# Dealing PSUM's eight banks anew: two for scores and four for the ring, in place of three and three

## The reference, cut to what matters

```python
mod = (silu(c) @ wmod).reshape(4, 6, 1, -1)
sa, ca, ga, sb, cb, gb = (mod[:, i] for i in range(6))      # ga, gb kept at least 0.25 from zero
h = layernorm(x) * (1 + ca) + sa
qkv = (h @ W_qkv + b_qkv), split by head into q, k, v
q, k = rope(q), rope(k)
att = softmax(causal(q @ k.T / sqrt(32)))
x = x + ga * ((att @ v) @ W_proj + b_proj)
h = layernorm(x) * (1 + cb) + sb
x = x + gb * ffn(h)
```

## Time and profile before

| what | value |
|---|---|
| runs: median (lowest to highest of 3) | 3261.88 us (3260.14 to 3275.57) |
| profiled execution: its own time, its span | 3263.36 us, 3261.6 us |
| mean granted TensorE clock | 0.969 |
| TensorE busy | 3008.8 us, 92% |
| VectorE busy | 2491.3 us, 76% |
| ScalarE busy | 1842.8 us, 57% |
| GpSimd busy | 1586.5 us, 49% |

### The profile page before, as it was taken

How to read it: one execution, slowest core, us unless ns; L and a number is a source line. 1 busy time by engine, 2 the same in 40 slices (tenths; PEclk the granted TensorE clock), 3 DMA queues, 4 the chain that set the end, 5 groups by cost and what they waited for, 6 DMA issues and landing times.

```text
span 3261.6 us, 59116 instructions
## 1 busy us (share of the span) xinstructions
PE 3008.8 (92%) x21664; PEld 1157.1 (35%) x21664; DVE 2491.3 (76%) x4214; ACT 1842.8 (57%) x3651; POOL 1586.5 (49%) x1586
## 2 busy tenths in 40 slices
PE   3699999999999999999999999999999999999896
PEld 1324343434343332434333243433424333342222
DVE  4597777777768788777877878777887878878477
ACT  2406565786655555786555555587555555455541
POOL 2303435382516556272654726366472645627355
PEclk8759999999999999999999999999999999999997
DMA  5403030413031120413114031321314122031121
GB/s 209 110 1 73 14 77 14 99 43 73 17 99 38 47 78 27 103 45 84 44 43 104 30 96 34 68 65 32 97 33 118 40 49 67 28 78 46 56 79 61
DMA packets 180875, 205.27 MB, mean 63 GB/s; under 512 B 21460, under 2 KB 137428, under 8 KB 179428
## 3 DMA queue, kind: packets, MB, share of 16 engines
q1 hardware_dynamic: 180584, 201.50, 23.1%
HBM read 114.09 MB, written 36.50 MB: 46 GB/s over the span
## 4 chain that ended last, share of the span: by engine, by line
PE 41%; issue 20%; DVE 13%; POOL 11%; POOLq 7%; ACT 3%; DVEq 2%; DMA 2%; SPq 1%; ACTq 1%
PE ring L1171 8%; PE ps_out L1221 8%; DVE mpart L911 8%; PE ps_scores L1207 7%; POOL psum L538 5%; PE ps_scores L1145 5%; PE ps_den L1238 4%; PE ps_den L1244 3%; POOL psum L537 3%; PE ring L1193 2%; PE ps_scores L1157 2%; POOLq L573 2%; POOLq L511 2%; POOLq L565 1%; ACT prob L739 1%
## 5 line engine op out<-in xcount | busy, mean ns | idle before, releaser
L739 ACT ACTIVATE prob<-ps_scores 128x512 f32<-128x512 f32 (+3 forms) x2560 | 1251.8, 537 | 950.1 <-PE ps_scores L1210 457.6
L911 DVE TENSOR_REDUCE mpart<-ring 128x1 f32<-128x512 f32 (+3 forms) x2560 | 1406.3, 599 | 356.6 <-PE ring L1171 191.0
L1171 PE MATMUL ring<-qk 96*128 96x512 f16 (+3 forms) x2560 | 875.0, 364 | 64.6 <-DVE mpart L911 46.7
L1207 PE MATMUL ps_scores<-qk 98*128 98x512 f16 (+3 forms) x2560 | 861.9, 350 | 44.4 <-ACT prob L739 36.2
L537 POOL TENSOR_TENSOR psum<-prob 128x512 f32<-128x512 f32 x360 | 480.6, 1335 | 387.2 <-ACT prob L739 305.7
L1221 PE MATMUL ps_out<-prob,v 128*32 128x512 f32 (+3 forms) x5120 | 602.0, 542 | 0.0
L1171 PEld LDWEIGHTS ring<-qk 96*128 96x128 f16 x2560 | 235.5, 98 | 857.6 <-DVE mpart L911 590.2
L538 POOL TENSOR_TENSOR psum<-prob 128x512 f32<-128x512 f32 x360 | 480.4, 1334 | 0.0
L1207 PEld LDWEIGHTS ps_scores<-qk 98*128 98x128 f16 x2560 | 245.8, 98 | 362.7 <-ACT prob L739 227.1
L1145 PE MATMUL ps_scores<-hT,wg 128*128 128x512 f16 x1536 | 346.1, 382 | 4.6 <-POOL hT L528 3.5
L556 POOL TENSOR_TENSOR xs<-xs,bc 128x512 f32<-128x512 f32 x60 | 81.0, 1350 | 432.0 <-DMA xs<-in_L_attn_x_dram 430.7
(11 more groups left out here) (128 smaller groups left out, 2581.9 us busy)
## 6 DMA issues: line engine op xcount, KB each, us to landing
qk<-half SPq DMA_DIRECT2D x384, 128.0 KB, 3.5
turn<-in_rope_dram SPq DMA_DIRECT2D x64, 512.0 KB, 4.6
xs<-in_L_attn_x_dram SPq DMA_DIRECT2D x124, 256.0 KB, 2.8
attn_out_T<-ot SPq DMA_DIRECT2D x63, 256.0 KB, 2.2
otin<-attn_out_T SPq DMA_DIRECT2D x30, 512.0 KB, 4.5
out_dram<-x SPq DMA_DIRECT2D x60, 256.0 KB, 2.1
wg<-w_qkv_halves SPq DMA_DIRECT2D x16, 768.0 KB, 5.1
qk<-in_L_wmod_dram SPq DMA_DIRECT2D x1, 6144.0 KB, 26.8
```

The source lines that it names most:

```text
L739: act.activation(prob[:, s % 3, p, h % 2, 0:w], ps_scores[(HG * s + h) % NBK][:, 0:w], ACT.Exp, scale=SCALE).then_inc(exp_done, 1)
L911: dve.tensor_reduce(mpart[:, h, qt, kc:kc + 1], ring[use % NBK][:, 0:w], AX.X, ALU.max).then_inc(ring_free, 1)
L1171: mm = pe.matmul(ring[use % NBK][:, 0:w], qk[0:R, G % 2, 0, h, qt * P:(qt + 1) * P], qk[0:R, G % 2, 1, h, kc * QC:kc * QC + w], start=True ...
L1207: mm = pe.matmul(ps_scores[k % NBK][:, 0:w], qk[0:RM, par, 1, h, kt * P:(kt + 1) * P], qk[0:RM, par, 0, h, cq * QC + q0:(cq + 1) * QC], st ...
```

## The change

Score k now goes into `ps_scores[k % 2]` and waits for the exponential of score k - 2. The ring has four banks: use n takes `ring[n % 4]` and waits for use n - 4. The values of `v_job` go into `ring[3]`, the bank `VB`; so in `qkv` a `bank_free` for the use that had this bank last stands ahead of the first chunk's `v_job`, and the wait for the evacuation of the last chunk's values moves from the third score of a group's first step to the first unit of the group that uses `ring[3]` (for the first group, ahead of its first unit). The modulation products at the start use the same eight banks under the new names.

```diff
-        NBK = 3
-        ps_scores = [ctx.enter_context(nc.psum_tensor(f"ps_scores{i}", [P, QC], F32)) for i in range(NBK)]
+        NSB, NBK = 2, 4
+        ps_scores = [ctx.enter_context(nc.psum_tensor(f"ps_scores{i}", [P, QC], F32)) for i in range(NSB)]
...
-        mod_banks = ps_scores + [ps_out, ps_den, ring[2]]
+        mod_banks = ps_scores + [ps_out, ps_den, ring[2], ring[3]]
+        VB = NBK - 1
...
-                            act.activation(prob[:, s % 3, p, h % 2, 0:w], ps_scores[(HG * s + h) % NBK][:, 0:w], ACT.Exp,
+                            act.activation(prob[:, s % 3, p, h % 2, 0:w], ps_scores[(HG * s + h) % NSB][:, 0:w], ACT.Exp,
...
-                                         ps_scores[2][:].rearrange("p (t n) -> p t n", t=TPC), 1.0 / W_SCALE, bias,
+                                         ring[VB][:].rearrange("p (t n) -> p t n", t=TPC), 1.0 / W_SCALE, bias,
...
-            def qkv(G, before):
+            def qkv(G, before, n):
...
                     if c == 0 and before is not None:
                         turn_maxima(before)
+                        bank_free(n + (VB - n) % NBK)
                     v_job(G, c)
...
-                            mm = pe.matmul(ps_scores[2][:, (t % TPC) * P:(t % TPC + 1) * P], hT[:, a, k, t * P:(t + 1) * P],
+                            mm = pe.matmul(ring[VB][:, (t % TPC) * P:(t % TPC + 1) * P], hT[:, a, k, t * P:(t + 1) * P],
...
-                pe.wait_ge(exp_done, wait_value(HG * NS * G + (k - NBK + 1 if k >= NBK else 0)))
-                mm = pe.matmul(ps_scores[k % NBK][:, 0:w], qk[0:RM, par, 1, h, kt * P:(kt + 1) * P],
+                pe.wait_ge(exp_done, wait_value(HG * NS * G + (k - NSB + 1 if k >= NSB else 0)))
+                mm = pe.matmul(ps_scores[k % NSB][:, 0:w], qk[0:RM, par, 1, h, kt * P:(kt + 1) * P],
...
-            qkv(0, None)
+            qkv(0, None, 0)
+            pe.wait_ge(v_evac, NC_)
...
-                        qkv(G + 1, G)
+                        qkv(G + 1, G, n)
...
+                    first_use = n
...
-                                if s == 0 and place == 2 and nxt:
-                                    pe.wait_ge(v_evac, NC_ * (G + 2))
                                 scores(G, par, s, place)
...
                                 u, h = units[place]
+                                if n % NBK == VB and n - first_use < NBK:
+                                    pe.wait_ge(v_evac, NC_ * (G + 2))
                                 unit_scores(G + 1, h, u, n)
```

More of the change, by code:

```diff
@@ L278, in adaln_block_kernel @@
             freed.append(counts[who])
-        assert NC_ == 4 and NBK == 3
+        assert NC_ == 4 and NBK == 4
         def job(G, c, kind):
@@ L1204, in scores @@
                 k = HG * s + h
-                pe.wait_ge(exp_done, wait_value(HG * NS * G + (k - NBK + 1 if k >= NBK else 0)))
-                mm = pe.matmul(ps_scores[k % NBK][:, 0:w], qk[0:RM, par, 1, h, kt * P:(kt + 1) * P],
+                pe.wait_ge(exp_done, wait_value(HG * NS * G + (k - NSB + 1 if k >= NSB else 0)))
+                mm = pe.matmul(ps_scores[k % NSB][:, 0:w], qk[0:RM, par, 1, h, kt * P:(kt + 1) * P],
                                qk[0:RM, par, 0, h, cq * QC + q0:(cq + 1) * QC], start=True, stop=not diag)
                 if diag:
-                    mm = pe.matmul(ps_scores[k % NBK][:, 0:P], identb[:], mask_kq[:], start=False, stop=True)
+                    mm = pe.matmul(ps_scores[k % NSB][:, 0:P], identb[:], mask_kq[:], start=False, stop=True)
                 mm.then_inc(scores_done, 1)
```

## The result

The changed kernel took 3348.94 us (median of 4 runs, 3344.78 to 3351.20), the kernel before in the same comparison 3264.96 us. The ratio is 1.0255, with a 95% interval of 1.0238 to 1.0271: slower by 84 us. I had forecast 3371 us, so +108, and a range of 3300 to 3435.

A forecast was written before the change was run, and what follows sets the result against it. TensorE was taken to lead the chain with 41%, other engines leading in stretches. Late scores of 271 us, less 47, 43, 18, 35 and 20, gave +108 on 3263.4, so 3371 us; range 3300 to 3435.

The forecast's parts named there:

- the ring's gain: Fourth bank's saving on ring waits: 43 us behind the third score in full, 18 us, a quarter of 73, ahead.
- Late scores: Scores waiting for exponential k - 2: 488 of 640 steps late by 271 us; 47 us only pass from score 3.
- the sum's 20 us for backlogs counted twice: Deduction for ScalarE backlogs counted in two steps, and for stretches where GpSimd or VectorE sets the end; bounds 0 and 81 us.
- The bound of 116 us: Most the fourth ring bank could save: main-stretch waits of units, projections and head tiles for their bank's last reader.
- Covered waits: 35 us of waits at places 2 to 4, mostly for pair sums, covered by the new delay; 20 us costing nothing.
- The last group, 26 us late: Late scores in the last group, which has no units between scores: 26 of the 271 us; group about 20 us longer.
- The other edits at nothing: The added `bank_free`, moved evacuation wait, first units' deeper ring and modulation products were to cost nothing; first units no different.
- The ring wins: Ring waits of 116 us and 35 us others vanish, late scores cost only 114: -37, 3226 us; chance 0.08.
- The waits cover one another: Only the last group pays about 20 us, the rest 0 to 40: 3283 to 3323 us; chance 0.12.
- Little is covered: Ring's gain stays at its quarter, score waits at places 0 to 2 add: +162 or more, 3425 to 3480 us; chance 0.09.
- The clock falls: New waits drop TensorE's clock to 0.66 in the last group: +69 us more, 3440 us; chance 0.03.
- The group from 1528 us: Group with output projections; if it got no longer, the prediction was wrong and its ring waits were worth more than allowed.

The follow-up runs named there:

- values first: The changed kernel with the values of the step before moved ahead of the third score (fourth in steps that open a query block): 3267.0 us.
- three scores, ring of three, shared bank: Kernel before with denominators added into the values' bank and the freed bank left empty (output not the reference's): 3269.0 us.
- three scores, ring of four, shared bank: Kernel before with denominators added into the values' bank and the freed bank given to the ring (output not the reference's): 3196.0 us.
- short pair sums: GpSimd's pair sums over 128 of 512 columns (output not the reference's): 3194.0 us in the kernel before, 3318.2 us in the changed kernel.

## Why the prediction was right, and where its terms were off

The direction and the size held, and so did the main mechanism. TensorE reaches the third score of a step 0.88 us behind the first, and its bank is free after 1.08 us. The trace after has 1.08 us in the step that I priced, and 1.07 in the last group. Lengthening the distance (values first) took the price to 6 us, and shortening the exponential took it to 19 us. The single terms fit less well than their sum, and that the total of 108 came within 24 us of the 84 is in part luck. The runs split it so: without the ring's gain my sum is 169 us (271 - 47 - 35 - 20), and two score banks beside a ring of three cost 128; the ring's gain I had at 61 us, and it was 44. One is 41 us too high, the other 17, and the second error hides part of the first.

A second walk shows where. It takes the lower quartile of a pair's distances as the usual one, and lists the denominators apart. It stands 13 to 14 us lower at scores than the walk of the prediction and 20 to 40 lower at units; its differences are what counts. Totals in us, from the first score on:

| kernel | scores | units, projections, head tiles | denominators |
|---|---|---|---|
| before (3 and 3) | 63 | 148 | 210 |
| two scores, ring of three | 249 | 118 | 171 |
| changed (2 and 4) | 295 | 34 | 171 |
| three scores, ring of three, shared bank | 63 | 149 | 212 |
| three scores, ring of four, shared bank | 96 | 40 | 225 |

- *Late scores, 271 us, less 47 us moved from score 3, so 224.* The changed kernel's +233 by the first walk looks like a hit, and is not one. The term priced the scores against a ring of three, and there they grew by 186 us (63 to 249): it was some 38 us too high, of which the sum's 20 us for backlogs counted twice were to take a part. The other 46 us (249 to 295) are what the fourth ring bank handed over to the scores. The parts are off as well. Place 2 grew by 183 us where I had 249, places 0 and 1 grew by 48, and score 3 gave up nothing (47 to 50), where I had taken 47 us off.
- *The ring's gain, 43 + 18 = 61 us.* Units, projections and head tiles wait 84 us less with the fourth bank (118 to 34), and scores 46 us more; the runs have 44 us for the two together. The bound of 116 us was not reached even beside three score banks, where the bank is worth 70 to 73. The reason that the earlier trace rows gave, that the wait moves to the next unit, is not what the walk shows: 109 of the 149 us went, and scores (+33) and denominators (+13) took part of that back. That ring and scores take from one another was right; 26 to 29 us is what they take (70 to 73, less 44).
- *Covered waits, 35 + 20 us.* Beside a ring of three the units' waits fell by 30 us and the denominators' by 39, 69 in all, so this step was some 14 us too small. The walk resolves the runs' 128 us to 11 us (186 - 69 = 117). The short pair sums agree that much is covered: with GpSimd out of the way the price is 124 us, so about 40 are covered with it, on that comparison. How the cover divides between VectorE and GpSimd stays open, since the probe changed GpSimd alone.
- *The groups' starts.* The walk behind my 271 us took ScalarE's delays as they stood in the old trace, but I named only its copies and its waits for GpSimd as their causes, not its casts for the next group (line 690). A third of the groups' growth, 32 of 94 us, lies in their first two steps. Short exponentials leave it (33 us), short pair sums nearly so (28), and the values moved ahead take it away (3). The timeline above shows the cast waiting for a DMA in one group; that it is the cause in all of them is not shown.
- *The last group, 26 us late.* It grew by 18.2 us, near the 20 I used.
- *The other edits at nothing.* True for the wait of the values' evacuation (2.3 us of load waits) and for `bank_free`. Not quite for the first units: from the first unit to the first score the kernel before took 120.7 us and the changed one 116.7. The first score comes at 259.7 us, where it came at 264.8; the other 1.1 us are an earlier start. Over the kernels here that stretch is 120.5 to 120.7 us with a ring of three, 116.7 to 119.3 with a ring of four and 140.4 with a ring of two. I had taken VectorE's 107.3 us of 119 for full.

The rivals: *The ring wins* is out by its own condition, since the scores cost 128 to 154 us. *The waits cover one another* has a part, and my sum had a little too little of it. *Little is covered* did not come. *The clock falls* did not come as I had priced it, a last group at 0.66: it was at 0.98 from 3137 to 3301 us. But I was wrong to read 1.00 over the main stretch as a clock that short waits leave alone. It fell in both kernels, for 89 us in the changed one and 34 before, and the mean over the run is 0.963 against 0.969. Compared pair by pair with the distances at full clock, the products in those stretches took at most 25 us longer in the changed kernel and 11 before, so I estimate the clock's part of the price at up to 14 us. The section "A second HAM failure mode: psum-queue depth-cycling" of the page "TensorE: Matmul & The Clock Gate" in the Trainium skill describes a swing of the clock where TensorE idles briefly between groups of matmuls. The trace agrees in that the changed kernel has such falls, among them the one at 983 us behind an idle time of 3.96 us. None of its falls between the first and the last score lasts longer than 10.2 us.

Of my signs, the loads' waits for ScalarE grew by 368 us over the whole run where I said 250, and those of unit loads fell by 136, where I said 40 to 100. Both rows also hold streaming time of the product before, so they are a poor measure of either. The first two groups grew by 6.7 us each, not 9. The group from 1528 us, whose growth was to be the test of the ring's worth, grew by 6.9.

## What to carry to other kernels

A buffer's worth is read by comparing, for each use, the time at which the consumer of the use before last would have freed it with the time at which the producer came; the producer's order of work sets that distance as much as the number of buffers does. Where two buffers must serve, put the longest other work between the uses that share a buffer (here one move was worth 82 us in the changed kernel and 6 in the kernel before). Two rings fed by one in-order engine are priced together: what one saves, the other waits for, so the worth of a bank must be read beside the deal it would stand in. And look at everything that the reading engine has in its queue: a cast that waits for a DMA holds back the exponential behind it, and with one bank less TensorE feels that sooner.

## What was not expected of the hardware

The idle time of a weight load behind a group of `values` is put down to ScalarE even where the array was busy throughout: moving the values raised the score loads' wait for ScalarE by 173 us (595.0 to 767.7) while the kernel got 82 us faster. ScalarE's exponential of 256 columns took 383 ns and of 512 columns 597 ns in the median, so half the columns save 0.21 us. A mean granted clock of 0.99 can hold 14 falls to 0.50.
